# Attention with normalised queries and keys: the gammas put on the normalised q by VectorE instead of into the weights

## The reference

```
q  = layernorm(x) @ Wq.T + bq          # per head: 8 features
kv = ctx @ Wkv.T + bkv                 # k and v, interleaved
q  = q * rsqrt(mean(q^2) + eps) * q_gamma     # per head
k  = k * rsqrt(mean(k^2) + eps) * k_gamma
x  = x + softmax(q k^T / sqrt(8)) v
x  = x + round(gelu_pwl(round(layernorm(x) @ w1 + b1)) @ w2 + b2)
```

## Time and profile before

| | |
|---|---|
| median of 3 runs | 209.04 us (208.56 to 210.41) |
| the profiled execution | 210.93 us |
| its span in the profile | 209.1 us |
| granted TensorE clock, mean | 0.982 of full speed |
| TensorE matmul busy | 184.6 us, 88% |
| VectorE busy | 186.9 us, 89% |
| ScalarE busy | 148.2 us, 71% |
| GpSimd busy | 117.8 us, 56% |

### The profile page before, as it was taken

One profiled execution on the slowest core, in us unless ns is written; L12 is line 12 of the kernel. 1 busy time (PEld: TensorE's weight loads), 2 busy tenths in 40 slices (PEclk: granted clock), 3 DMA queues, 4 the chain that ended last, 5 costly groups with the idle time before them and its releaser, 6 DMA issues.

```text
span 209.1 us, 8050 instructions
## 1 busy us (share of the span) xinstructions
PE 184.6 (88%) x3324; PEld 141.1 (67%) x3324; DVE 186.9 (89%) x348; ACT 148.2 (71%) x228; POOL 117.8 (56%) x164
## 2 busy tenths in 40 slices
PE   6857899899999999999899799869899999984693
PEld 2446788688888887888788546356567666553692
DVE  6978998979999998989899777999999999999882
ACT  5134787687777887689677779967878888878411
POOL 7537557766768677686664501474444565644530
PEclk9999999999999999999999999999999999999679
DMA  3363111011101111011000000000101101010103
GB/s 90 109 192 85 55 53 36 22 53 53 55 19 41 53 55 53 6 28 31 3 3 3 3 5 3 0 0 0 53 6 45 50 0 53 0 50 0 50 3 100
DMA packets 14836, 7.97 MB, mean 38 GB/s; under 512 B 1072, under 2 KB 14576, under 8 KB 14800
## 3 DMA queue, kind: packets, MB, share of 16 engines
q1 hardware_dynamic: 14272, 7.20, 12.2%
q10 hardware_dynamic: 528, 0.25, 0.4%
HBM read 5.35 MB, written 2.10 MB: 36 GB/s over the span
## 4 chain that ended last, share of the span: by engine, by line
PE 46%; DVE 22%; POOL 13%; issue 12%; DMA 3%; SPq 1%; ACT 1%; DVEq 0%; POOLq 0%
POOL y_raw L398 8%; PE bank_o L1047 8%; PE banks_p L1017 8%; PE banks_p L985 6%; PE banks_s L1031 5%; DVE frac L834 5%; DVE banks_p L841 4%; PE banks_p L999 4%; PE bank_o L1057 4%; DVE y_raw L849 3%; PE banks_p L981 3%; DVE act_q L855 2%; DMA c_in<-in_ctx_dram 2%; PE banks_p L951 2%; DVE seg L828 2%
## 5 line engine op out<-in xcount | busy, mean ns | idle before, releaser
L398 POOL TENSOR_TENSOR y_raw<-g_lo,y_raw 128x1024 f32<-128x1024 f32 x15 | 35.5, 2364 | 34.2 <-DVE frac L834 33.2
L455 ACT ACTIVATE probs<-banks_s 128x512 f32<-128x512 f32 x64 | 33.0, 609 | 1.3 <-PE banks_s L1031 1.3
L1169 PEld LDWEIGHTS bank_o<-w,act_q 128*128 128x128 f32 x224 | 28.8, 205 | 7.2 <-DVE act_q L855 7.0
L1169 PE MATMUL bank_o<-w,act_q 128*128 128x128 f32 x224 | 30.4, 293 | 1.8 <-DVE act_q L855 1.5
L334 POOL TENSOR_TENSOR parts<-qk_hat,parts 128x512 f16<-128x512 f32 x16 | 18.6, 1161 | 22.3 <-DVE parts L630 22.3
L1154 PE MATMUL banks_s<-x2T,w 128*128 128x512 f32 x60 | 30.6, 592 | 0.0
L516 ACT ACTIVATE g_lo<-seg,gelu_lo 128x1024 f32<-128x1024 f32 x16 | 18.4, 1150 | 8.4 <-DVE seg L828 8.4
L525 ACT ACTIVATE banks_p<-seg,gelu_hi 128x1024 f32<-128x1024 f32 x16 | 17.9, 1118 | 6.8 <-DVE y_raw L849 6.8
L1017 PE MATMUL banks_p<-ident,parts 128*128 128x128 f16 x256 | 19.6, 219 | 2.2 <-POOL parts L334 1.8
L1047 PE MATMUL bank_o<-probs,v_blk 128*32 128x64 f32 x1024 | 20.7, 222 | 0.0
L849 DVE SCALAR_TENSOR_TENSOR y_raw<-banks_p,frac 128x1024 f32<-128x1024 f32 x16 | 19.6, 1224 | 0.6
(11 more groups left out here) (115 smaller groups left out, 426.6 us busy)
## 6 DMA issues: line engine op xcount, KB each, us to landing
x_all<-in_x_dram SPq DMA_DIRECT2D x16, 128.0 KB, 2.6
c_in<-in_ctx_dram SPq DMA_DIRECT2D x16, 128.0 KB, 2.2
out_dram<-x_all SPq DMA_DIRECT2D x7, 256.0 KB, 2.3
w<-in_L_ffn_w_dram SPq DMA_DIRECT2D x2, 256.0 KB, 3.2
out_dram<-x_all SPq DMA_DIRECT2D x2, 128.0 KB, 1.9
b_rows<-in_L_ffn_b_dram SPq DMA_DIRECT2D x1, 192.0 KB, 3.5
wkv_raw<-in_L_xattn_Wkv_dram ACTq DMA_DIRECT2D x1, 128.0 KB, 2.9
bkv_rep<-in_L_xattn_bkv_dram SPq DMA_DIRECT2D x1, 128.0 KB, 4.5
```

Source lines behind the costliest of these rows:

```text
L398: g.tensor_tensor(y_raw[u][:], g_lo[n % 3][:], y_raw[u][:], ALU.add).then_inc(S[f"gelu{u}_done"], 1)
L455: a.activation(probs[i][:].rearrange("p t g n -> p (t g n)"), bank_s(i), ACT.Exp).then_inc(S["probs_ready"], 1)
L1169: last = t_.matmul(out, act_q[u][:, c, P * t:P * t + P], w2[:, CH // UNITS * u + c, :], start=False, stop=(u == UNITS - 1 and t == GT - 1 ...
```

## The change

The query is projected once, without gammas, together with k into bank_qk. VectorE multiplies the normalised q in qk_hat by gqk, in place, with a new instruction between normalise and highs (scale_q). The scaled weights wqgT, the scaled bias, the second q projection into bank_in and its bias matmul are gone, and the bias tile has no scaled part any more. ScalarE squares bank_qk as one piece. Two waits of TensorE for the squares are gone, since bank_in no longer holds a q. The guard loop is changed in the same way.

```
-        wqgT = sb("wqgT", [P, DIM])
...
-        B_Q, B_QG, B_K, B_1, B_2, B_END = 0, DIM, 2 * DIM, 3 * DIM, 3 * DIM + FF, 4 * DIM + FF
+        B_Q, B_K, B_1, B_2, B_END = 0, DIM, 2 * DIM, 2 * DIM + FF, 3 * DIM + FF
...
             def square(s):
                 wait(act, "qk_proj", s + 1)
                 wait(act, "ms_ready", s)
-                a.activation(qk_sq[:].rearrange("p w t d -> p w (t d)"),
-                             banks_p[:, 256:1280].rearrange("p (w r) -> p w r", w=2)[:, :, 0:2 * DIM], ACT.Square).then_inc(S["qk_squared"], 1)
+                a.activation(qk_sq[:].rearrange("p w t d -> p (w t d)"), bank_qk, ACT.Square).then_inc(S["qk_squared"], 1)
...
+            def scale_q(s):
+
+                wait(dve, "qk_normed", s + 1)
+                q = qk_hat[:, 0, :, :].rearrange("p t (h d) -> p (t h) d", d=DH)
+                v.tensor_tensor(q, q, gqk[:].unsqueeze(1).to_broadcast([P, 2 * HEADS, DH]), ALU.mult).then_inc(S["q_scaled"], 1)
+
             def highs(s):
...
-                wait(dve, "qk_normed", s + 1)
+                wait(dve, "q_scaled", s + 1)
...
                     normalise(s + 1)
+                    scale_q(s + 1)
                     highs(s + 1)
...
-            dve.wait_ge(S["wq_ready"], 2)
-            v.tensor_tensor(wqgT[:].rearrange("p (h d) -> p h d", d=DH), wqT[:].rearrange("p (h d) -> p h d", d=DH),
-                            gqk[:].unsqueeze(1).to_broadcast([P, HEADS, DH]), ALU.mult).then_inc(S["w_ready"], 1)
...
-            setup(v.tensor_tensor(b_rows[:, B_QG:B_K].rearrange("p (h d) -> p h d", d=DH), b_rows[:, B_Q:B_QG].rearrange("p (h d) -> p h d", d=DH),
-                                  gqk[0:BR, :].unsqueeze(1).to_broadcast([BR, HEADS, DH]), ALU.mult), then=False)
...
             def transpose_in(s, par):
...
-                wait(pe, "qk_squared", s)
...
                 wait(pe, "in_t_copied", s + 1)
-                if not first:
-                    bias_q()
                 for t in range(2):
-                    t_.matmul(bank_in[:, DIM * (2 + t):DIM * (3 + t)], xcT[:, 0, t, :], wqT[:], start=(first and t == 0), stop=(t == 1 and not first))
-                for t in range(2):
-                    for which, w in ((0, wqgT[:]), (1, wkT[:].rearrange("p h d -> p (h d)"))):
+                    for which, w in ((0, wqT[:]), (1, wkT[:].rearrange("p h d -> p (h d)"))):
...
             def project_v(s):
 
                 wait(pe, "in_t_copied", s + 1)
-                wait(pe, "qk_squared", s + 1)
```

More of the change, by code:

```diff
@@ L121, in xattn_ffn @@
         b_rest = sb("b_rest", [BR, B_END])
-        b_parts = sb("b_parts", [P, B_END], F16)
+        b_parts = sb("b_parts", [P, B_END + DIM], F16)
         x_all = sb("x_all", [P, TOKENS])
@@ L198, in xattn_ffn @@
             x_loaded c_loaded c_free ln_stats ln_var ln_rstd xn_centred xn_ready
-            in_t in_t_copied qk_proj qk_squared ms_ready ms_logged rms_ready qk_normed
+            in_t in_t_copied qk_proj qk_squared ms_ready ms_logged rms_ready qk_normed q_scaled
             hi_ready shift_ready lo_ready parts_t parts_t_copied0 parts_t_copied1 scores_ready probs_ready v_proj v_evac
@@ L202, in xattn_ffn @@
             bound_sq_ready g_done g_loaded g_stats g_moments g_var g_rstd g_centred g_xn g_in_t g_in_copied
-            g_qk g_squared g_ms g_logged g_rms g_normed  g_high g_parts_t g_parts_copied g_scores g_max
+            g_qk g_squared g_ms g_logged g_rms g_normed g_scaled  g_high g_parts_t g_parts_copied g_scores g_max
             ln2_stats ln2_var ln2_rstd xn2_ready x2_t x2_t_copied h_first hz_first h_proj hz_ready
@@ L477, in guard @@
                 act.wait_ge(S["g_qk"], t + 1)
-                a.activation(qk_sq[:, 0, :, :],
-                             banks_p[:, 256:1024].rearrange("p (w r) -> p w r", w=2)[:, :, 0:DIM], ACT.Square).then_inc(S["g_squared"], 1)
+                a.activation(qk_sq[:, 0, :, :].rearrange("p t d -> p (t d)"), bank_qk[:, 0:2 * DIM], ACT.Square).then_inc(S["g_squared"], 1)
                 act.wait_ge(S["g_ms"], t + 1)
@@ L766, in guard @@
                 dve.wait_ge(S["g_normed"], t + 1)
+                v.tensor_tensor(hat[:, 0:HEADS, :], hat[:, 0:HEADS, :], gqk[:].unsqueeze(1).to_broadcast([P, HEADS, DH]),
+                                ALU.mult).then_inc(S["g_scaled"], 1)
+                dve.wait_ge(S["g_scaled"], t + 1)
                 for which in range(2):
@@ L963, in bias_qk @@
                 def bias_qk():
-                    t_.matmul(bank_qk.rearrange("p (w t d) -> p w t d", w=2, t=2), pick16[:],
-                              b_parts[:, B_QG:B_1].rearrange("p (w d) -> p w d", w=2).unsqueeze(2).to_broadcast([P, 2, 2, DIM]),
+                    return t_.matmul(bank_qk.rearrange("p (w t d) -> p w t d", w=2, t=2), pick16[:],
+                              b_parts[:, B_Q:B_1].rearrange("p (w d) -> p w d", w=2).unsqueeze(2).to_broadcast([P, 2, 2, DIM]),
                               start=not first, stop=first)
[L968 to L974, removed]
+                if not first:
                     wait(pe, "qk_normed", s)
@@ L987, in project_qk @@
                     pe.wait_ge(S["bqk_ready"], 1)
-                    bias_qk()
-                    last = bias_q()
+                    last = bias_qk()
                 last.then_inc(S["qk_proj"], 1)
@@ L1084, in weights_ready @@
                 pe.wait_ge(S["wq_ready"], 2)
-                pe.wait_ge(S["w_ready"], 9)
+                pe.wait_ge(S["w_ready"], 8)
                 pe.wait_ge(S["bqk_ready"], 1)
@@ L1096, in guard @@
                 weights_ready()
-                bias(bank_qk[:, 0:2 * DIM], B_QG, 2 * DIM, 1)
+                bias(bank_qk[:, 0:2 * DIM], B_Q, 2 * DIM, 1)
                 pe.wait_ge(S["g_in_copied"], t + 1)
-                bias(bank_in[:, 2 * DIM:3 * DIM], B_Q, DIM, 1)
-                t_.matmul(bank_in[:, 2 * DIM:3 * DIM], xcT[:, 0, 0, :], wqT[:], start=False, stop=True)
-                t_.matmul(bank_qk[:, 0:DIM], xcT[:, 0, 0, :], wqgT[:], start=False, stop=False)
+                t_.matmul(bank_qk[:, 0:DIM], xcT[:, 0, 0, :], wqT[:], start=False, stop=False)
                 t_.matmul(bank_qk[:, DIM:2 * DIM], xcT[:, 1, 0, :], wkT[:].rearrange("p h d -> p (h d)"),
```

## The result

The changed kernel takes 215.34 us in the median (215.06 to 216.83, 5 runs) against 209.04 before: ratio 1.030, interval 1.025 to 1.035, so 6.3 us slower. The forecast was slower, 213.2, range 210.6 to 215.4: the direction, the mechanism and the step of 6.85 us were right, the total was 2.1 us short. The time is inside the range by only 0.06 us, and outside the narrower one of the forecast itself, 212.0 to 214.3; that it fell inside at all is luck.

A forecast was written before the change was run, and what follows sets the result against it. A loop of dependences through VectorE, GpSimd and TensorE was taken to bound the 6.40 us attention step; +0.90, +2.63, +0.2 and +0.45 gave +4.2, so 209.04 became 213.2 us, range 210.6 to 215.4 (own range 212.0 to 214.3).

The forecast's parts named there:

- TensorE waits for GpSimd in an undisturbed step; the step is a loop of 6.40: Attention stage: TensorE waits about 0.1 us for GpSimd's low parts; dependences through three engines make the 6.40 us step.
- Price 0.45: Added scale_q on VectorE between normalise and highs: 0.42 us long plus 0.03 hand-over, bounds 0.36 to 0.50.
- the margin of 0.14: GpSimd's inverse root ends 0.14 us before scale_q starts, so no stretch costed; port rival: 219 us, chance 0.04.
- The removed TensorE work is worth nothing in an undisturbed step: Bias matmul and q projection, 0.56 us per step, lie ahead of the turning of parts, outside the loop: worth nothing.
- VectorE alone needs 6.25 to 6.33: VectorE's own need per attention step before the change, from its idling of 0.07 to 0.15 us in 6.40.
- The rival built on it: Only VectorE's occupancy counts in the attention steps: 6.70 a step, +2.0, 211.0 us; chance 0.14.
- Setup and first scale_q cost nothing: Before 16.7 us: about 1 us saved on VectorE becomes idling before a DMA, hiding step 0's scale_q; both zero.
- the one of the twelve steps: Attention stage, 33.80 to 113.37: twelve steps of 6.85 make 82.20 against 79.57, +2.63, if TensorE's slack swallows the stalls.
- 0.9 + 5.4 + 0.45: Forecast terms: two scale_q from 16.7 to 33.8, +0.90; twelve steps, forecast as +2.63; step 15's scale_q, +0.45.
- The stalls stay in the loop, 215.3: Rival: TensorE's stalls in the attention steps aren't swallowed, another 2.1 us on top, 215.3 us; chance 0.10.
- The +0.2 for stalls left over: Twelve attention steps: stalls TensorE's slack doesn't swallow, between 0 and 2.3 us, taken as +0.2.

The follow-up runs named there:

- the loop is stretched by 0.07: Changed kernel with GpSimd multiplying the gammas onto the inverse root, VectorE normalising q with that product, no scale_q: 209.47 us, ratio 1.001 to the kernel before.
- the instruction off the loop: Changed kernel with scale_q moved behind the attention output, its result written to a tile nobody reads: 211.81 us, ratio 1.012 to the kernel before, steps of 6.66.
- The second profile of the kernel before: Kernel before run again unaltered: median 209.52 us, ratio 1.002; the profiled execution took 209.42 us.
- the first profile of the changed kernel: Profiled execution of the changed kernel's first run, the slowest of five: 216.83 us.
- in the second profile: Changed kernel run again unaltered: median 214.67 us, ratio 1.030 to the kernel before; the profiled execution took 214.21 us.

## Why the prediction was right, and where its size was off

- *TensorE waits for GpSimd in an undisturbed step; the step is a loop of 6.40.* Shown: 6.40 with and without TensorE's removed work, 6.86 with scale_q on either base, 6.47 when the loop is stretched by 0.07. The 0.25 from the low parts' end to the matmul, on which the reading rested, is there in most steps after (the others below).
- *Price 0.45.* 0.46 by the step; 0.42 long, 0.03 on each side. GpSimd's inverse root ended at 71.07 and scale_q started at 71.21: the margin of 0.14 was as worked out, and none of the 16 instructions was stretched (0.42 to 0.43).
- *The removed TensorE work is worth nothing in an undisturbed step.* Shown, by taking scale_q out and by putting it into the kernel before.
- *VectorE alone needs 6.25 to 6.33.* Near enough: 6.21, by the instruction off the loop. The rival built on it (6.70 a step) is out, since in the loop the loop decides.
- *Setup and first scale_q cost nothing.* Right for the changed kernel (w1's scaling at 16.79 against 16.71, after 1.02 us of idling), but the two cancel: with the old setup kept, the first scale_q pushes GpSimd's low parts and with them the end of w1's scaling back, and the first copy of parts by 0.56.
- **The term that failed** is the one of the twelve steps: +2.63, from 12 x 6.85 less 79.57. That a slack of 1 us swallows a stall was right (shown for one stop, above). What was wrong was to count the 2.8 us of stalls of one profile as a saving for the median execution too. The second profile of the kernel before, at 209.42 close to the median, has none, and against it the term is 12 x 0.45 = 5.4 (5.56 measured). Then the sum is 0.9 + 5.4 + 0.45 = 6.75, 215.8 us; 215.3 was measured. The warning stood in the text: that execution lay 1.9 above the median. It lay no higher because it had no drop of the clock near the end of the stage: that cost the second profile 1.3 us, and 2.8 less 1.3 is the 1.5 us between the two executions. How much stalling the median execution holds, three profiles don't say; the interval (5.2 to 7.2 us slower) leaves room for up to 1.5 beside the 6.75.
- *The stalls stay in the loop, 215.3.* The number is the measured one, by chance: steps of 6.85 rule it out.
- The +0.2 for stalls left over: five of the twelve steps in the first profile of the changed kernel are 6.95 to 7.02, because L1006 started 0.35 to 0.42 behind L333 instead of 0.25; one step in the second profile. Its cause is open.

## What to carry to other kernels

An engine that is busy all the time need not be the one that sets the pace. Before crediting matmuls taken away, measure whether the full engine's first instruction in a step starts when the one ahead of it lets it, or a fixed time behind another engine's result (here 0.25 us); a loop of dependences can hide behind it, and the chain of waits didn't name it here. If the profiled execution lies above the median, find what makes it so (here steps that break the pattern) before subtracting anything from it; taking the pattern step as the base would have given 215.8. And work moved off a full engine should go to one with a pause, at a place where its result is not yet awaited: on GpSimd the multiplication by the gammas cost 0.07 us a step, on VectorE in the loop 0.46.

## What the runs showed of the hardware

- Two executions of one program differ in TensorE's waits for nothing that the profile names: 2.1 us in three, none, and 2.2 us in five waits, in three profiles of the kernel before. Where they come, they come at the same matmuls.
- The granted clock fell to half, its lower level of 1.2 GHz, for 3.4 us in most cases, early in the attention stage and once more around or behind its end in some executions of a program and not in others (kernel before: none, both, both; changed: both, none); a further one, between 193 and 208 us, is in all twelve profiles. At the end of the stage this cost 1.1 us in the changed kernel, 1.3 in the one before.
- The two-input VectorE instruction took 0.42 us in the loop and 0.79 (0.62 where it started later) beside GpSimd's subtraction, ending 0.28 behind that each time, and GpSimd's next took 0.91 instead of 0.73. The Trainium skill (SBUF — State Buffer, section "SBUF: two separate sides") describes such a lock, held for a whole instruction, between a VectorE operation with two SBUF inputs and a GpSimd one; the trace agrees, with these 0.37 and 0.18 us.
- GpSimd hands a result to TensorE in 0.25 us (L333's end to L1006; 0.35 to 0.42 in some steps), VectorE to itself in 0.03.
